# One exponential operation of 1600 columns for each chunk of keys in place of two of 800, in the cross attention of a decoder layer

## The reference

```python
scores = jnp.einsum('bhsr,bhlr->bhsl', q_r, k_r)
attn = jax.nn.softmax(scores, axis=-1)
ctx_c = jnp.einsum('bhsl,bld->bhsd', attn, kv_r)
ctx_lat = jnp.einsum('bhsd,hkd->bhsk', ctx_c, w_kc_kv)
ctx = ctx_lat.transpose(0, 2, 1, 3).reshape(Bv, Sv, H * K)
return ctx @ Wo.T
```

## Time and profile before

| | |
|---|---|
| time, median of 3 runs | 2326.58 us (2323.96 to 2330.46) |
| time of the profiled execution | 2327.78 us |
| its span, first to last instruction | 2325.9 us |
| mean granted TensorE clock | 0.970 |
| PE busy | 2203.7 us, 95% |
| DVE busy | 1684.9 us, 72% |
| ACT busy | 1200.1 us, 52% |
| POOL busy | 1828.5 us, 79% |
| exponentials L1809 | 768 instructions, 602.0 us |
| sums L1779 | 347 instructions, 1138.6 + 115.7 us |

### The profile page before, as it was taken

How to read it: one execution, slowest core, us unless ns; L and a number is a source line. 1 busy time by engine, 2 the same in 40 slices (tenths; PEclk the granted TensorE clock), 3 DMA queues, 4 the chain that set the end, 5 groups by cost and what they waited for, 6 DMA issues and landing times. The chain is left out here.

```text
span 2325.9 us, 47164 instructions
## 1 busy us (share of the span) xinstructions
PE 2203.7 (95%) x15390; PEld 1410.0 (61%) x15390; DVE 1684.9 (72%) x2755; ACT 1200.1 (52%) x1949; POOL 1828.5 (79%) x818
## 2 busy tenths in 40 slices
PE   7989859999996999999999999999999999999798
PEld 4545557777773555555555555555655555555587
DVE  6888858888875677677677677667677667767775
ACT  4333232232223666666666666666666666666243
POOL 3554547988982899999999999999999999999211
PEclk9889979999995999999999999999999999999999
DMA  5001024666666334324324424334333333431011
GB/s 186 22 15 28 15 65 142 189 183 194 175 197 149 89 90 88 97 69 96 97 66 100 97 66 100 88 75 94 86 83 84 86 93 75 91 92 40 25 44 41
DMA packets 239504, 216.15 MB, mean 93 GB/s; under 512 B 124500, under 2 KB 213768, under 8 KB 239304
## 3 DMA queue, kind: packets, MB, share of 16 engines
q1 hardware_dynamic: 239432, 215.22, 36.4%
HBM read 129.68 MB, written 60.78 MB: 82 GB/s over the span
## 5 line engine op out<-in xcount | busy, mean ns | idle before, releaser
L1779 POOL TENSOR_TENSOR x_acc<-x_acc,x_prob 128x1600 f32<-128x1600 f32 x315 | 1138.6, 3615 | 26.2 <-ACT x_prob L1809 2.3
L1809 ACT ACTIVATE x_prob<-x_scores 128x800 f32<-128x800 f32 (+1 forms) x768 | 602.0, 837 | 19.5 <-PE x_scores L2114 8.9
L2147 PE MATMUL x_context<-x_prob,x_kv 128*64 128x400 f32 x2816 | 550.5, 512 | 7.0 <-ACT x_ctxs L1849 6.7
L1916 DVE TENSOR_REDUCE x_mx<-x_ring 115x2 f32<-115x1024 f32 x310 | 380.1, 1226 | 30.0 <-PE x_ring L2214 9.8
L1925 DVE TENSOR_REDUCE x_mx<-x_ring 115x1 f32<-115x466 f32 (+3 forms) x352 | 221.9, 630 | 243.1 <-PE x_ring L2221 242.6
L1829 ACT COPY x_half<-x_ring 115x466 f32<-115x466 f32 (+3 forms) x352 | 190.0, 540 | 332.4 <-PE x_ring L2221 332.3
L2147 PEld LDWEIGHTS x_context<-x_prob,x_kv 128*64 128x64 f32 x2816 | 171.3, 136 | 241.4 <-issue 235.9
L2114 PE MATMUL x_scores<-x_qh,x_dh 64*128 64x400 f32 (+1 forms) x1536 | 272.7, 350 | 0.3 <-ACT x_prob L1809 0.3
L2114 PE MATMUL x_scores<-x_qh,x_dl 64*128 64x400 f32 (+1 forms) x1536 | 266.9, 342 | 0.0
L2114 PE MATMUL x_scores<-x_ql,x_dh 64*128 64x400 f32 (+1 forms) x1536 | 266.7, 341 | 0.0
L1929 DVE TENSOR_REDUCE x_mx<-x_half 115x1 f32<-115x466 f32 (+3 forms) x352 | 220.3, 626 | 4.3 <-ACT x_half L1829 1.1
(11 more groups left out here) (212 smaller groups left out, 3692.0 us busy)
## 6 DMA issues: line engine op xcount, KB each, us to landing
scratch_qh<-q_qsh SPq DMA_DIRECT2D x64, 200.0 KB, 3.2
scratch_ql<-q_qsl SPq DMA_DIRECT2D x64, 200.0 KB, 3.5
x_qm<-scratch_qh SPq DMA_DIRECT2D x64, 200.0 KB, 3.6
x_qh<-scratch_qh SPq DMA_DIRECT2D x64, 200.0 KB, 3.4
x_ql<-scratch_ql SPq DMA_DIRECT2D x64, 200.0 KB, 3.7
x_rden<-scratch_rden SPq DMA_DIRECT2D x64, 200.0 KB, 3.5
scratch_kr<-q_krot SPq DMA_DIRECT2D x32, 384.0 KB, 2.3
x_kr<-scratch_kr SPq DMA_DIRECT2D x32, 384.0 KB, 4.7
```

Source lines behind the costliest of these rows:

```text
L1779: pool.tensor_tensor(acc[0:rows, parity], first, prob[0:rows, c % PR], ALU.add).then_inc(acc_done.sem, 1)
L1809: act.activation(prob[0:rows, c % PR, u * HALF:(u + 1) * HALF].rearrange("p (j s) -> p j s", j=2), psc[0:rows, u, :, 0:BANK], ACT.Exp).the ...
L1916: dve.tensor_reduce(best[0:block_rows(r), :, r, i], src[0:block_rows(r), :, 0:b - a], AX.X, ALU.max).then_inc(read_sem(u), 1)
L2147: mm = pe.matmul(pav[DC * s:DC * s + DC, j, 0:BANK], kv[0:rows, parity, c], prob[0:rows, c % PR, cols], start=c == 0, stop=c == LC - 2)
```

## The change

The helper `exponentials` loses its argument `u`. It issues one activation over the four banks of `psc` for a chunk, once both halves' scores are there, and adds 2 to `exp_done` at its end. The waits for the place in `prob` are as before. PE's, POOL's and DVE's code is unchanged, so the counts that they wait for are unchanged too.

```diff
-            def exponentials(n, c, u):
+            def exponentials(n, c):
                 rows = rows_of(c)
 
-                if u == 0:
-                    act.wait_ge(av_done.sem, av_done.at(n, c - 3))
-                    if is_at(n, B - 1) and c - PR in (5, 6):
...
+                act.wait_ge(av_done.sem, av_done.at(n, c - 3))
+                if is_at(n, B - 1) and c - PR in (5, 6):
...
-                act.wait_ge(s_filled.sem, s_filled.at(n, 2 * c + u + 1))
-                act.activation(prob[0:rows, c % PR, u * HALF:(u + 1) * HALF].rearrange("p (j s) -> p j s", j=2),
-                               psc[0:rows, u, :, 0:BANK], ACT.Exp).then_inc(exp_done.sem, 1)
+                act.wait_ge(s_filled.sem, s_filled.at(n, 2 * c + 2))
+                act.activation(prob[0:rows, c % PR].rearrange("p (b s) -> p b s", b=4),
+                               psc[0:rows, :, :, 0:BANK].rearrange("p u j s -> p (u j) s"),
+                               ACT.Exp).then_inc(exp_done.sem, 2)
...
-                        for u in range(2):
-                            exponentials(n, c, u)
+                        exponentials(n, c)
```

More of the change, by code:

```diff
@@ L1795, in _ @@
                 act.sem_inc(rg.read[i], rg.credit("read", i))
-            def exponentials(n, c, u):
+            def exponentials(n, c):
                 rows = rows_of(c)
-                if u == 0:
-                    act.wait_ge(av_done.sem, av_done.at(n, c - 3))
-                    if is_at(n, B - 1) and c - PR in (5, 6):
[L1803 to L1807, removed]
-                act.wait_ge(s_filled.sem, s_filled.at(n, 2 * c + u + 1))
-                act.activation(prob[0:rows, c % PR, u * HALF:(u + 1) * HALF].rearrange("p (j s) -> p j s", j=2),
-                               psc[0:rows, u, :, 0:BANK], ACT.Exp).then_inc(exp_done.sem, 1)
+                act.wait_ge(av_done.sem, av_done.at(n, c - 3))
+                if is_at(n, B - 1) and c - PR in (5, 6):
+                    act.wait_ge(late_sums.sem, 1)
+                elif is_at(n, B - 1) and c - PR > 6:
+                    act.wait_ge(acc_done.sem, acc_done.at(n, pool_sums.index(c - PR) + 1))
+                else:
+                    act.wait_ge(acc_done.sem, acc_done.at(n, max(c - 4, 1) if c >= PR else c - 3))
+                act.wait_ge(s_filled.sem, s_filled.at(n, 2 * c + 2))
+                act.activation(prob[0:rows, c % PR].rearrange("p (b s) -> p b s", b=4),
+                               psc[0:rows, :, :, 0:BANK].rearrange("p u j s -> p (u j) s"),
+                               ACT.Exp).then_inc(exp_done.sem, 2)
             def copy_turn(n, parity, i):
```

## The result

| | before | after |
|---|---|---|
| median | 2325.98 us (2323.96 to 2330.46, 4 runs) | 2365.38 us (2363.81 to 2372.25, 4 runs) |
| profiled execution, its span | 2327.78, 2325.9 us | 2364.25, 2362.3 us |
| mean granted TensorE clock | 0.970 | 0.974 |
| ratio | | 1.0174, 95% interval 1.0157 to 1.0191 |

The change makes the kernel slower by 39.4 us by the medians and by 36.4 us from span to span. The forecast was 28.2 us slower, 2354.8, with a range of 2342 to 2365; the measured median lies just above the range. The sign was right and so were the two delays forecast for PE. A third delay, by way of POOL, was missing, and the amount was too small by 8 to 11 us.

What follows compares the result with a forecast made beforehand. PE was taken to bound the kernel, busy 43.91 of 44.24 us per item. The terms 29 x 0.90 + 2 x 0.56 + 1.0 = 28.2 us slower gave 2354.8 us on the median; range 2342 to 2365.

Steps and rivals of the forecast that it cites:

- The cost of the new operation: ACT's one exponential of 1600 columns per chunk: 1.52 us, bounds 1.40 to 1.67, against 1.56 or 1.57 for two.
- Rival B: The merged exponential takes 1.67 us, making PE 1.20 us late per item: 37.8 us slower, 2364.4; chance 0.10.
- Middle chunks (3 to 10) cost nothing: PE's maximum and context products cover the longer exponential, with 0.15 us of cover left, so no delay.
- Chunk 0 to 1: Only the small context product covers chunk 0's exponential, so PE stands 0.75 us before loading the next scores.
- Chunk 1: PE's context product had idled 0.27 us for L1849; that wait is swallowed, leaving PE 0.48 us late.
- Chunk 2 to 3: Exponential 0.97 us later delays ACT's copies, DVE's L1892 and PE's half product L2221: PE 0.90 us late in all.
- Rival A: Chunk 2's copies or PE's timing hide the second 0.42 us; PE is 0.48 late: 15.9 us slower, 2342.5; chance 0.10.
- POOL comes 0.56 later there and PE 0.90, so POOL's margin grows and it doesn't bind: At the item's end, before PE's output product, POOL's margin of 0.25 us was to grow, leaving PE to set the item.
- Rival R: In the follow-ups, no chance given: only PE's own lateness counts, the rest of 1.23 us per item comes from elsewhere.
- The last item: Without half products, its tail hangs on POOL and moves with chunk 1's exponential: at least 0.56 us, taken as 1.0.
- Rival C: ACT's own time is on the path in every chunk, so merging gives back 15 us, 2311; chance 0.04.
- Rival D: PE's stall makes TensorE's clock fall to 0.74 for the whole phase: about 480 us on top, 2800; chance 0.02.

## Why the prediction was wrong

The step that failed is POOL's: it was forecast to come 0.56 us later and not to bind, and it came 1.35 us later and set the item. That is one of the signs of being wrong that the prediction names itself, "if L2204 waits for POOL in most items". The steps one by one:

- **The cost of the new operation** (1.52 us): 1.504 measured, right. Rival B with 1.67 us is out, though its total of 2364.4 lay nearest to the result; that is a coincidence.
- **Middle chunks (3 to 10) cost nothing:** right for chunks 4 to 11, shown by the kernel with chunks 0, 2 and 3 restored. From chunk 3 to 11 PE needs 25.7 us in both kernels. It is wrong for chunk 3: PE's products do cover its longer operation, but POOL's third sum doesn't. The kernel that merges chunk 3 besides (chunks 0 and 2 restored) takes 44.54 us per item, the one without it 44.22.
- **Chunk 0 to 1** (0.75 us): 0.80, right. **Chunk 1:** 0.27 was to be swallowed and 0.48 left; 0.40 was swallowed and 0.40 left. Shown alone by the kernel with only chunk 0 merged.
- **Chunk 2 to 3** (PE late by 0.90): 0.90, right, partly by luck. The exponential of chunk 2 ended 0.92 later and not 0.97, and nothing came off behind it, since L1818 began 0.51 us after L1843 as before and not 0.4. Rival A, without this link, is excluded by the kernel with only chunk 2 merged.
- **"POOL comes 0.56 later there and PE 0.90, so POOL's margin grows and it doesn't bind":** this step failed. I took POOL's lateness from chunk 1's exponential, with which its chain starts, and treated all later sums as running without a gap. They did before the change, but the third with only 0.06 us in hand. That sum waits for chunk 3's exponential, which is late by PE's 0.90 and by another 0.50 of its own. POOL's scaled context came 1.35 us later, ate the 0.17 in hand at L2204 (0.25 in the prediction) and set the item: 1.23 us on average and not 0.90. The 0.33 us over 27 ordinary items is 9 us. In the two items near the end, where POOL was the bound before, the loss was 1.17 us each and not 0.56, which is 1.2 us more. Rival R is refuted by four kernels: two restore chunks and still find the POOL wait, and two relieve POOL and find 45.12 us.
- **The last item** (1.0 us): mis-sized. Its last output product starts 54.7 us behind the last mark before and 56.5 after, 1.8 later:

```profile
L2204 PE MATMUL x_ring<-x_wco,x_ctxn x530: 379/379/634, 750.0 to 2182.3; 128*100 128x256 f32 x177
```

```profile
L2203 PE MATMUL x_ring<-x_wco,x_ctxn x530: 379/379/634, 747.1 to 2218.9; 128*100 128x256 f32 x177
```

The forecast path is there: DVE waited 4.74 us for POOL as before and started L2009 1.40 us later behind the mark, 2175.97 - 2162.44 against 2139.72 - 2127.59. But without half products the cover is short in the other chunks too, not in chunk 0 alone: PE waited for the exponential 8 times, 2.5 us together, and before once, 0.3. No run separates the two.

```profile
2165.95 1.50 ACT L1808 ACTIVATE x_prob<-x_scores 128x1600 f32<-128x1600 f32 x1 [0.82 <-PE x_scores L2113]
```

```profile
2175.97 3.55 DVE L2009 SCALAR_TENSOR_TENSOR f_shift<-f_mv,f_rstd 100x4 f32<-100x4 f32 x1 [4.74 <-POOL f_rstd L1783]
```

```profile
PE x_scores L2113 <- ACT x_prob L1808: 2.5, 8, 0.8
```

- **Rival C** (ACT's time on the path) is out: fewer ACT operations in nine chunks changed nothing. Its sentence on 0.186 us per chunk leaves out that the same section of the Trainium skill lets activations one behind the other overlap; see the last section.
- **Rival D** (the clock) is out too: the granted clock of an item is 1.00 although PE idles 0.86 us in it. The 0.74 of the earlier trace rows was a mean over two levels, 0.50 from 706.3 to 757.5 and 1.00 around it, and PE was busy for 80% of that window against 98% of an item after the change:

```profile
706.30:757.50 51.20, 34.57 (x133) 16.99 (x135) 33.50 (x47) 17.16 (x34) 8.21 (x12) 0.50 0.66 163
757.50:800.00 42.50, 42.29 (x309) 25.15 (x311) 30.14 (x41) 26.72 (x40) 39.48 (x13) 1.00 0.31 70
```

The first item, 46.67 against 44.76 us from mark to mark, lost 0.7 us more than an ordinary one, and the second, 0.25 us longer than before, lost 1.0 us less. The cause of both stays open.

## What to carry to other kernels

Merging two operations on an engine with time to spare gained nothing here, and it delayed the first half's consumers and the release of the first half's buffer: look at what covers that delay at the places where the pipeline is short (the first chunk, a chunk with extra copies), not in the middle. When a chain on another engine runs without a gap, each of its steps has its own input; work out the time in hand at each of them, not only at the first, for the one with the least sets the chain once its input moves. Where the loop is regular, one item's length in a single profile resolved 0.05 us, while whole runs of unchanged code differed by some microseconds.

## What the runs showed of the hardware

Two exponentials of 800 columns in a row take 1.56 us and one of 1600 takes 1.504, so the merge itself is worth 0.06 us. From 837 and 1504 ns the slope is 0.834 ns a column. By the Trainium skill, "ScalarE: Activation LUTs", section "What ACT_TABLE_LOAD costs", an activation with immediate scale and bias takes 186 ns plus 0.833 ns a column, 1519 ns here by estimate, and two in a row overlap by about 93 ns. The slope agrees, and so does the overlap: two take 1.56 us and not 2 x 0.837, 0.11 less. By the figures of the Trainium skill merging would give back 186 - 93 = 93 ns, an estimate; 0.06 us was measured.

From the end of an exponential to the start of the sum that waited for it POOL took 0.08 us for the first sum of an item (1439.79 to 1439.87) and 0.16 for the third (1447.85 to 1448.01). The handover differs from step to step between the same two engines, so where the time in hand is as small as 0.06 us it has to be read at the very step. What makes the difference stays open.

Once per item PE's weight loads idled for 0.72 us and its products for 0.5 behind chunk 0's exponential, and the granted TensorE clock stayed at 1.00 in each item window that was read.
